# Expert stage of a gated attention and expert kernel: scatters and the first expert's split spread over shared steps, router columns stationary, three blocks of tokens loaded a stage ahead

## The reference, cut to what matters

```python
x = x + tanh(g_xattn[0]) * attention0(layernorm(x), ctx)      # stage "a_": l0_attention
x = x + tanh(g_ffn[0]) * ffn0(layernorm(x))                   # stage "b_": l0_experts
...
def ffn0(x):                          # T = 2048, H = 512, F = 352, E = 8, top 2
    scores = softmax(x @ gate_weight.T)
    topk_w, topk_idx = top_k(scores, 2)
    combine = zeros((T, E)).at[arange(T)[:, None], topk_idx].add(topk_w)
    gu = einsum('th,efh->tef', x, gate_up_weights)
    y = einsum('tef,te,ehf->th', silu(gu[..., :F]) * gu[..., F:], combine, down_weights)
    sgu = x @ shared_gate_up.T        # shared expert of width 2F, for all tokens
    return y + (silu(sgu[:, :2 * F]) * sgu[:, 2 * F:]) @ shared_down.T
```

## Time and profile before

| | us |
|---|---|
| median of 3 runs | 2206.16 (2204.09 to 2206.22) |
| profiled execution | 2200.77 |
| its span | 2199.0 |
| attention stage, from the start to the last store | 0 to 921 |
| expert stage | 921 to 1480 |
| of it, shared steps on PE | 949 to 1188.5 |
| of it, expert tiles on PE | 1208 to 1478 |

### The profile page before, as it was taken

The page is one execution under the profiler, slowest core; times in us unless marked ns, Lnnn a source line. Parts: engine busy times, 40 slices in busy tenths (PEclk is TensorE's granted clock), DMA queues, the critical chain, the costliest instruction groups (busy, mean ns, idle before and its releaser), DMA issues. The chain is left out here.

```text
span 2199.0 us, 30241 instructions
## 1 busy us (share of the span) xinstructions
PE 1969.6 (90%) x10428; PEld 1649.3 (75%) x10428; DVE 1017.7 (46%) x1561; ACT 826.7 (38%) x1578; POOL 1094.9 (50%) x805
## 2 busy tenths in 40 slices
PE   6999999999999999689996999985799874789998
PEld 5888788878887888478884899983677653568886
DVE  3556654755476547623331333335466343583111
ACT  3336332633363336231211222223377763233332
POOL 6755576557655774441147646606254222533332
PEclk9999999999999999879998999997899966899999
DMA  4232323133313331362326655427676635222000
GB/s 155 82 105 68 116 96 106 53 108 116 107 48 112 101 124 30 118 214 82 139 95 204 197 164 161 131 75 210 175 187 153 169 113 184 81 68 67 19 19 19
DMA packets 173869, 251.29 MB, mean 114 GB/s; under 512 B 45040, under 2 KB 69616, under 8 KB 173744
## 3 DMA queue, kind: packets, MB, share of 16 engines
q1 hardware_dynamic: 158656, 205.23, 30.0%
q0 software_dynamic: 9472, 34.09, 4.9%
q10 hardware_dynamic: 5616, 10.23, 1.2%
HBM read 182.92 MB, written 66.58 MB: 113 GB/s over the span
## 5 line engine op out<-in xcount | busy, mean ns | idle before, releaser
L238 POOL TENSOR_TENSOR a_w_hl<-a_w_raw,a_w_hl 128x2048 fp32r<-128x2048 f32 x65 | 299.8, 4613 | 164.6 <-ACT a_w_hl L300 164.4
L413 PE MATMUL a_proj<-a_c_hl,a_w_hl 128*128 128x512 f32 x768 | 183.2, 399 | 21.4 <-DVE a_w_hl L530 19.6
L300 ACT ACTIVATE a_w_hl<-a_w_raw 128x2048 fp32r<-128x2048 f32 x66 | 126.2, 1912 | 164.6 <-PE a_proj L413 106.7
L413 PEld LDWEIGHTS a_proj<-a_c_hl,a_w_hl 128*128 128x128 f32 x768 | 146.2, 192 | 53.8 <-issue 19.6
L487 PE MATMUL a_proj<-a_w_hl,a_a_hl 128*128 128x512 f32 x768 | 179.5, 392 | 4.0 <-DVE a_a_hl L586 4.0
L413 PE MATMUL a_proj<-a_w_hl,a_c_hl 128*128 128x512 f32 x768 | 181.3, 392 | 0.0
L413 PE MATMUL a_proj<-a_a_hl,a_w_hl 128*128 128x512 f32 x768 | 176.4, 390 | 0.0
L319 ACT ACTIVATE a_sq<-a_proj,a_vecs 128x512 f32<-128x512 f32 x128 | 87.9, 689 | 228.6 <-PE a_proj L413 149.1
L487 PEld LDWEIGHTS a_proj<-a_w_hl,a_a_hl 128*128 128x128 f32 x768 | 142.7, 188 | 34.3 <-POOL a_w_hl L238 5.5
L413 PEld LDWEIGHTS a_proj<-a_a_hl,a_w_hl 128*128 128x128 f32 x768 | 143.6, 188 | 29.7
L262 POOL TENSOR_TENSOR a_ssum<-a_ssum,a_sq 128x512 f32<-128x512 f32 x112 | 145.6, 1300 | 36.9 <-ACT a_sq L319 33.2
(11 more groups left out here) (245 smaller groups left out, 3682.5 us busy)
## 6 DMA issues: line engine op xcount, KB each, us to landing
a_w_raw<-in_a_ki_w SPq DMA_DIRECT2D x18, 1024.0 KB, 5.2
a_w_raw<-in_a_vi_w SPq DMA_DIRECT2D x16, 1024.0 KB, 5.1
a_w_raw<-in_a_q_w SPq DMA_DIRECT2D x16, 1024.0 KB, 5.1
a_w_raw<-in_a_o_w SPq DMA_DIRECT2D x16, 1024.0 KB, 5.4
b_gu_raw<-in_b_gate_up POOLq DMA_DIRECT2D x32, 352.0 KB, 3.7
l_sorted_rows<-b_zeros SPq DMA_DIRECT2D x39, 256.0 KB, 3.3
b_hs<-l_sorted_rows SPq DMA_DIRECT2D x39, 256.0 KB, 3.2
l_expert_out<-b_yg ACTq DMA_DIRECT2D x39, 256.0 KB, 3.5
```

Of the source, the lines that this page charges most:

```text
L238: pool.tensor_tensor(w_hl[:, s, 1], w_raw[:, s], f32(w_hl[:, s, 0]), ALU.subtract)\
L300: act.activation(w_hl[:, i % 2, 0], w_raw[:, i % 2], ACT.Copy).then_inc(w_high, 1)
L413: mm = pe.matmul(proj[:, j, :], left, right, start=(k == 0 and n == 0), stop=(k == KC - 1 and n == 2))
```

## The change

1. `carry` is allocated before the attention stage, whose tensor `v` now lies in it. The loops of the attention stage run 3 turns, and the last block is written out behind them, without the loads and splits for a next block. In it SP loads the x1 rows of blocks 0 to 2 into `carry` once the attention of the last block has been done. The expert stage loads block 3 alone, behind the weights of half 0.
2. The router columns are stationary and the tokens move: 12 matmuls per block. The result, 8 x 512, is copied by DVE to `raw_logit`, turned by PE with 4 transposes, and taken. `take_logits` and `choose` come behind the third product of a step; `down` still waits for `logits_taken`.
3. `SCATTERED` ends two parts earlier, and expert 0 is split between the low parts of step 7 (`FIRST_SPLIT`). Its first loads are issued at the end of step 6.

```diff
@@ l0_attention, SP
+                    if last and i == O0 + 1:
+                        sp.wait_ge(av_ready, NU * NBLK)
+                        for b in range(NBLK - 1):
+                            for j in range(TPB):
+                                sp.wait_ge(x_out[j], 16 * NBLK)
+                            sp.dma_start(y_next[:, TPB * b:TPB * (b + 1), :], x1_b[b]).then_inc(next_in, 16)
...
-            with sp.Fori(0, NBLK) as t:
+            with sp.Fori(0, NBLK - 1) as t:
+                block_of_tokens(t, False)
+            block_of_tokens(NBLK - 1, True)
@@ l0_attention, POOL (ACT's w_high_part likewise)
-                    else:
+                    elif i + 2 < NW or not last:
                         w_low(NW * t + i + 2, (i + 2) % NW)
@@ l0_experts
-    SCATTERED = (0, 2, 6, 10, 14, 18, 22, 26, 29, 32)
+    SCATTERED = (0, 4, 9, 14, 19, 24, 28, 32, 32, 32)
+    FIRST_SPLIT = ((0, 1), (2, 3), (4, 5, 6))
@@ SP
-            for b in range(NBLK):
-                if b:
-                    sp.dma_start(y[:, b * TPB:(b + 1) * TPB, :], x1_t[b]).then_inc(x_in[b], 16)
...
-                    load_weights(0, E, 0)
+            sp.dma_start(r_raw[:], W["router"].rearrange("(k p) e -> p k e", p=P)).then_inc(const_in, 16)
+            sp.dma_start(gate[:], W["gate"].to_broadcast([P, 1])).then_inc(const_in, 16)
+            sp.sem_inc(gu_split, 2)
+            sp.sem_inc(dn_split, 2)
+            load_weights(0, E, 0)
+            sp.dma_start(y[:, (NBLK - 1) * TPB:, :], x1_t[NBLK - 1]).then_inc(x_in, 16)
@@ POOL
+                    if step == SHARED - 2 and f == NF - 1:
+                        pool.wait_ge(gu_split, KC * 2 + 2)
+                        pool.wait_ge(dn_split, NF * 2 + 2)
+                        for n in range(AHEAD):
+                            load_chunk(n)
                     if step == SHARED - 1:
-                        if f == 0:
...
-            for n in range(NC):
-                split_chunk(n)
-                load_chunk(n + AHEAD)
+                        for n in FIRST_SPLIT[f]:
+                            split_chunk(n)
+                            load_chunk(n + AHEAD)
@@ ACT
-                    if f == 1 and step == 2 * (NBLK - 2):
+                    if step == SHARED - 1:
+                        if f == 0:
+                            act.wait_ge(y_ready, TPB * (SHARED - 1))
+                        for c in FIRST_SPLIT[f]:
+                            first_high(c)
+                    if f == NF - 1 and step == SHARED_RANK - 1:
                         act.wait_ge(route, 2)
                         act.activation(left[:], left[:], ACT.Exp).then_inc(exp_ready, 1)
@@ PE
             def logits(b):
+                if b == 0:
+                    pe.wait_ge(r_split, 1)
                 pe.wait_ge(h_split, TPB * (b + 1))
+                for k in range(KC):
+                    for m, (wp, ap) in enumerate(PASSES):
+                        mm = pe.matmul(y_ps[0:E, 0, :], r_hl[:, wp, k, :], h_hl[:, b % 2, ap, k, :],
+                                       start=(k == 0 and m == 0), stop=(k == KC - 1 and m == 2))
+                mm.then_inc(logits_ready, 1)
+
+            def turn_logits(b):
+                pe.wait_ge(logits_copied, b + 1)
                 for j in range(TPB):
-                    for k in range(KC):
-                        for m, (wp, ap) in enumerate(PASSES):
...
+                    mm = pe.transpose(y_ps[:, 1, j * E:(j + 1) * E], raw_logit[:, j * P:(j + 1) * P], ident[0:E, 0:E])
+                mm.then_inc(logits_turned, 1)
...
-            pe.wait_ge(r_split, 1)
             turn_block(0, 0)
...
                 gate_up(step, s, s, b % 2, 2)
                 if step == 0:
                     logits(b + 1)
+                if ahead:
+                    turn_logits(b + 1)
@@ DVE
+                ahead = s == 0 and b + 1 < NBLK
+                if step:
+                    product(step, s, 1)
+                    if ahead:
+                        copy_logits(b + 1)
+                product(step, s, 2)
                 if step == 0:
-                    product(step, s, 2)
+                    copy_logits(b + 1)
+                if ahead:
                     take_logits(b + 1)
-                else:
...
+                if step == SHARED_RANK - 1:
+                    choose()
```

More of the change, by code:

```diff
@@ L203, in _ @@
                 for i in range(NW):
-                    load_w(NW * t + i + 2, (i + 2) % NW)
+                    if i + 2 < NW or not last:
+                        load_w(NW * t + i + 2, (i + 2) % NW)
                     if i < 2:
@@ L249, in _, with block_of_tokens @@
             w_low(1, 1)
-            with pool.Fori(0, NBLK) as t:
+            def block_of_tokens(t, last):
                 def add_square(half, n):
@@ L286, in _ @@
                                 .then_inc(p_ready, 1)
-                            if u % 4 == 3:
+                            if u % 4 == 3 and not last:
                                 c_low(KC * t + KC, u // 4)
                         w_low(NW * t + i + 2, i + 2)
-                    else:
+                    elif i + 2 < NW or not last:
                         w_low(NW * t + i + 2, (i + 2) % NW)
+            with pool.Fori(0, NBLK - 1) as t:
+                block_of_tokens(t, False)
+            block_of_tokens(NBLK - 1, True)
         @block.scalar
@@ L309, in _, with block_of_tokens @@
             w_high_part(1, 1)
-            with act.Fori(0, NBLK) as t:
+            def block_of_tokens(t, last):
                 def square(i, j):
@@ L379, in _ @@
                         act.wait_ge(o_ready, TPB * t + TPB)
-                    if i != O0 - 1:
+                    if i != O0 - 1 and (i + 2 < NW or not last):
                         w_high_part(NW // 2 * t + (i + 2) // 2 + 1, i % 2)
@@ L387, in _ @@
                         attention()
+            with act.Fori(0, NBLK - 1) as t:
+                block_of_tokens(t, False)
+            block_of_tokens(NBLK - 1, True)
         @block.tensor
@@ L391, in _, with block_of_tokens @@
             pe.wait_ge(const_made, 3)
-            with pe.Fori(0, NBLK) as t:
+            def block_of_tokens(t, last):
                 def project(i, tiles=range(4)):
@@ L530, in _, with block_of_tokens @@
             dve.tensor_tensor(w_hl[:, 0, 1], w_raw[:, 0], f32(w_hl[:, 0, 0]), ALU.subtract).then_inc(w_split, 1)
-            with dve.Fori(0, NBLK) as t:
+            def block_of_tokens(t, last):
                 def normalise_x(j):
@@ L745, in l0_experts @@
         zeros_out = sem("zeros_out")
-        x_tile_in = [sem(f"x_tile_in{j}") for j in range(TPB)]
-        x_in = {b: sem(f"x_in{b}") for b in range(1, NBLK)}
+        x_in = sem("x_in")
         ln_stats = sem("ln_stats")
@@ L1063, in chunk, with first_high @@
                 a_high_part(step, par, f)
+            def first_high(c):
+                raw, _, arrived, w, hi, _ = expert_chunk(0, c)
+                width = D if hi >= DOWN else 2 * F
+                act.wait_ge(arrived, chunks_in(0, c))
+                act.activation(wts[0:w, 0, hi:hi + width], raw, ACT.Copy).then_inc(e_high, 1)
             h_high_parts(0, 0)
@@ L1105, in store_tile @@
                 act.dma_start(expert_out[i * P:(i + 1) * P, :], yg[:, i % 2, :]).then_inc(yg_out[i % 2], 16)
-            act.wait_ge(y_ready, TPB * (SHARED - 1))
-            for c in range(KC + NF):
-                first_high(c)
             x_high_part(0)
@@ L1425, in _ @@
                     assign()
+                ahead = s == 0 and b + 1 < NBLK
[4 more added lines that the diff above has]
+                product(step, s, 2)
                 if step == 0:
-                    product(step, s, 2)
+                    copy_logits(b + 1)
+                if ahead:
                     take_logits(b + 1)
-                else:
-                    product(step, s, 1)
-                    if s == 0 and b + 1 < NBLK:
-                        take_logits(b + 1)
-                    if step == SHARED_RANK - 1:
-                        choose()
-                    product(step, s, 2)
+                if step == SHARED_RANK - 1:
+                    choose()
                 for j in range(TPB):
@@ L2620, in stage @@
         last[0] = sems
-    stage(l0_attention, a["x"], a["ctxT"], part("a_"), x1)
     with nc.sbuf_tensor("place", [P, 2, T // P], I32) as place, \
@@ L2626, in build @@
             with nc.sbuf_tensor("carry", [P, T // P * D], F32) as carry:
+                stage(l0_attention, a["x"], a["ctxT"], part("a_"), carry[:], x1)
                 stage(l0_experts, x1, part("b_"), x_shared, rows, sorted_rows, expert_out, place, weight, carry[:],
```

52 lines of the change are left out of this document (28 added, 24 removed).

## The result

| | before | after |
|---|---|---|
| median (4 runs each) | 2205.12 us | 2182.23 us |
| lowest, highest | 2200.47, 2206.22 | 2176.93, 2184.07 |
| ratio to before | | 0.9901, 95% interval 0.9878 to 0.9925 |
| profiled execution, its span | 2200.77, 2199.0 | 2184.07, 2182.3 |

1.0% faster, and clear of the noise: the interval leaves out 1. 2183.6 was predicted for the median and 2178.2 for the profiled execution.

A forecast was written before the change was run, and what follows sets the result against it. PE was taken as the bound, busy 90% of the span. Terms -3.5 - 0.5 - 2.7 - 8.1 - 4.0 - 2.3 - 3.5 + 2 = -22.6 us gave a 2183.6 us median (2178.2 profiled), range 2174 to 2194.

The forecast's parts named there:

- Part 1, tail: End of the attention stage: without the useless POOL split the last DVE residual addition shortens, -3.5 us.
- The 0.5 for the parts dropped beside PE: Last attention block: dropping four context parts and two weight loads saves 0 to 3 us, taken as 0.5.
- rival (d): Attention stage: the unrolled last block is starved of instructions and the kernel is slower, up to 2228 us; chance 0.04.
- the 6 that were to show it: Sign of being right: gate_up of the expert stage starting some 6 us earlier in the span.
- Part 2, start: Start of the expert stage: transposes and weights' high parts start earlier, gate_up 2.7 us sooner, range 1.5 to 3.5.
- Part 3, step 0: First shared step: cheaper logits, fewer waits and full-rate down, 42.3 to 34.2 us, 8.1 less (5 to 10).
- gate_up of two chunks unchanged 13.9: Term of step 0's sum: the first two gate_up chunks keep their 13.9 us.
- Rival (c): Step 0 stays bound by the weights' chain, only the logits' 3 us gained: -17.5, 2188.5 us; chance 0.10.
- Part 4, steps 2 and 4: Logits to down takes 10.2 us each, including a new wait on the take: -4.0 and -2.3 us.
- Part 5: Scatters and first split, steps 5 to 7: tile loads 3.5 us sooner, clock loss +2 after new PE stops.
- rival (a): POOL queue paces worse, rows return late to hs and each stop halves the clock: -17.1, 2189 us; chance 0.18.
- at least 1 of those 2 us was lost: Clock price after a 2.66 us PE stop, from a 0.50 clock window; applied to the stops of steps 5 and 6.

The follow-up runs named there:

- e9: The kernel before, unchanged, profiled a second time: attention stage's last matmul ends at 913.44 us (911.75 in the first profile), step 0 takes 44.1 us.
- e8: Changed kernel whose last attention block again loads and splits two weight groups nobody uses: 2184.05 us (1 run), start of the expert stage 34.43 us.
- e10: Kernel before with only the changed attention stage, without its x1 loads, and carry placed earlier: 2198.75 us (1 run).
- e7: Changed kernel with the x1 loads put back into the expert stage: 2185.52 us (1 run), step 0 36.58 us.
- e6: Changed kernel with the old router product, tokens stationary, 48 matmuls of 8 columns per block: 2191.72 us (1 run), step 0 36.94 us.
- e4: Changed kernel with scatters and first split reordered so that PE does not stop for POOL: median 2173.12 us (4 runs), ratio 0.9871.
- e5: e4 plus DVE taking the logits ahead of product 2 in steps 2 and 4: median 2166.78 us (5 runs), ratio 0.9824.
- e3: Changed kernel with 12 unused 512-column matmuls filling each PE stop of steps 5 and 6: 2173.28 us (1 run), last stretch 92.31 us.
- e2: Changed kernel with one scatter less ahead of the last low parts of steps 5 and 6: 2171.74 us (1 run), last stretch 90.92 us.
- e1: Changed kernel with the old scatter order and first-expert split put back: 2185.02 us (4 runs), ratio 0.9919, last stretch 95.50 us.

## Why the prediction was right, and where its steps were off

The median was right to 1.4 us: 22.9 us of gain, 22.6 in the sum. Part of that is luck. Between the two profiled runs it is 16.7, and the sum for the profiled run was 5.9 us too low (2178.2 for 2184.07). The changed kernel's profiled run was the slowest of its four, and the first profile of before a good run of its kernel, in the attention stage and in step 0: against e9's marks the stretches of the changed kernel differ by +0.7, -6.0, -11.0, -6.2 and +2.4, together -20.1. So the median came out right because terms that were off by +2.9, -1.1 and +3.9 us met a pair of medians that lie 6 us further apart than the two profiles.

**Part 1, tail: right.** -3.5 predicted; e8 gives 3.3 back, e10 gains 3.3 to 3.5. The 0.5 for the parts dropped beside PE was not seen (the stage's end moves by 3.8 us between profiles, so it could not be). The 2 us allowed for the loads of x1 on SP's queue were not needed. Instruction supply, rival (d), is refuted: the last block's matmuls are as dense as the loop's, and e10's block is as long as e9's turn to 0.1 us. That gate_up of step 0 starts 3.9 us earlier in the span, and not the 6 that were to show it, is the +2.4 of the attention stage.

**Part 2, start: right.** -2.7 predicted, 6.26 less 3.3 to 3.5 measured, 2.8 to 3.0. e7 (31 us with late loads) and e6 (30.9 with the old router form) leave the moved wait for r_split as what is left of the edits there; it was not undone by itself.

**Part 3, step 0: 1.1 too small**, 33.14 us for 34.2 laid out. The chain that is new was laid out at 1.7 us and took 0.77 + 0.41 + 0.37 and little overlap, 1.6, though no row had given the 0.4 of the transposes. The term that was off is "gate_up of two chunks unchanged 13.9": from 945.31 to 958.37 it was 13.1, since the first chunk, in which the clock comes back up, took 7.12 us. In e4, with the same code in this step, that chunk took 8.46, and the step 34.48. So the miss is within what the same code does from profile to profile. The base moves too: step 0 of before is 42.3 us in one profile and 44.1 in another. Rival (c), that only the 3 us of the logits count there, falls with the result and with e7: with the late loads back the step is still 5.7 us shorter.

**Part 4, steps 2 and 4: right to 0.1 us**, in its parts as well: 12 matmuls 2.93, gate_up 5.64 from start to start, the wait 1.25. That the wait hangs on DVE's order, and not on the transposes, is e5's result.

**Part 5: the term that was mis-sized.** Laid out -3.5 for POOL and +2 for the clock, -1.5; measured +2.4 here, and +0.7 to +1.0 in e6, e7 and e8, which have the same order (96.2 to 96.5 us). The stops themselves were right to 0.4 us each. The scatters of a group started 1.27 to 1.30 us apart (1.54 once, at the first), so the first half of rival (a), rows that come back to hs late, is refuted. Its second half, that each stop halves the clock, is what steps 5 and 6 show, and its sum, -17.1, lay nearest to the profiles' -16.7. The failed step is "at least 1 of those 2 us was lost ... I take +2, range 0 to 4": it read the window of 2 us behind the stop and took one lost us for each of two stops. The kernel before had a fuller answer in the row behind that stop:

```profile
255.35 12.55 PE L413 MATMUL a_proj<-a_c_hl,a_w_hl 128*128 128x512 f32 x48
```

The three stops of this kind in its profile, 2.47 to 2.77 us, were followed by 12.55, 12.79 and 11.19 us for the same 48 matmuls, so they cost 1.4, 1.6 and nothing. One us a stop was a fair mean for that place; in steps 5 and 6 it was three times as much. Filling the stops (e3) gives back 5.6 us, beyond the range of 0 to 4, or 3.9 to 4.2 against e6 to e8. The lower clock holds through the 12 matmuls behind the stop (5.49 and 5.39 for 2.8) and into gate_up (17.25 and 17.63 for 16.8): 2.7 and 0.4, 2.6 and 0.8, so 3.1 and 3.4 us; in e6 to e8 it is 3.2 to 3.4 for the first stop and 1.8 for the second. As POOL's next input is dated by PE, the delay comes back on POOL: before its first low part of step 6 it waited 7.38 us in the changed kernel, 4.51 in e3 with the same order, and 5.98 in the kernel before.

```profile
1133.01 1.28 POOL L972 TENSOR_TENSOR b_a_hl<-b_prod,b_a_hl 128x512 fp32r<-128x512 f32 x1 [7.38 <-ACT b_a_hl L1083]
```

**Attention: +2.4 where -0.5 stood**, the clock at the start of a block, which the profile of before had at its best.

## What to carry to other kernels

When work is moved under PE's cover on another engine, lay it out against the time at which PE wants each result, and put the long runs where PE has its longest stretch of its own work: the same 32 scatters and 7 splits cost 97.9, 95.5, 90.9 or 84.6 us by their order alone. A stop of PE of 2 to 3 us ahead of dense work is to be priced at its length and 0 to 3.4 us more, and the upper end belongs in the range. And since the totals of one kernel spread by 4 to 13 us here, cut the timelines at marks that both kernels have: the stretches repeat to 0.1 us where the clock does not move, and show what the total hides.

## What the runs showed of the hardware

- After the stops of PE of 1.94 to 2.96 us in steps 5 to 7 the next 12 matmuls of 512 columns took 3.9 to 5.5 us instead of 2.8, with the granted clock at 0.50 behind the stop of step 5, but 3.03 us once, after 2.94 us in step 7 of e2. After 1.69 us they took 4.61, after 0.69 and 0.81 there was no fall (3.06, 3.02). Twelve matmuls whose result nobody reads kept it at 1.00.
- The fall is not the same each time: the same 48 matmuls behind the stop at 703 took 11.2 us in two profiles and 12.7 to 13.7 in ten, and one of the two (e3) had a stop of 3.17 us, as long as any.
- 48 matmuls of 8 columns, each with its own 128-column stationary operand, brought the clock from 0.94 to 0.50 with PE busy throughout. The Trainium skill (TensorE: Matmul & The Clock Gate, What's actually happening) calls the half rate the resting state that activity releases; in these rows PE did not rest before it fell.
- A DVE addition of 0.69 us took 4.21 beside one POOL subtraction of 4.58, and a DVE subtraction of 1.08 took 6.07 beside four in a row, in one profile of e1 and not in the changed kernel's at the same distance of 0.28 us.
